# Two-layer graph network on one core: sums of sub-blocks for the second layer formed two units ahead instead of one

## What is computed

```python
def _L0_gnn_ref(h, adj, W_neigh, b_neigh, W_self, b_self):
    deg = jnp.sum(adj, axis=1, keepdims=True) + 1e-05
    h_neigh = (adj / deg) @ h
    return relu(h_neigh @ W_neigh.T + b_neigh + h @ W_self.T + b_self)

def _L1_gnn_ref(x, adj, W, b):
    rowsum = adj.sum(axis=1)
    d = jnp.where(rowsum > 0, rowsum ** (-0.5), 0.0)
    return relu((d[:, None] * adj * d[None, :]) @ x @ W + b)

x = layernorm(x + _L0_gnn_ref(x, adj, ...))      # x: 4096 x 256, adj: 4096 x 4096, all fp32
x = layernorm(x + _L1_gnn_ref(x, adj, ...))
```

## Time and profile before

| | |
|---|---|
| Median of three runs | 785.76 us |
| The profiled execution's own time | 786.03 us |
| Its span, first to last instruction | 784.3 us |
| TensorE, matmul | 769.7 us busy (98%) |
| VectorE (DVE) | 719.4 us busy (92%) |
| ScalarE (ACT) | 422.7 us busy (54%) |
| DMA | 161.09 MB, mean 205 GB/s |
| Granted TensorE clock, mean | 0.995 |

### The profile page before, as it was taken

One profiled execution on the slowest core, in us unless ns is written; L12 is line 12 of the kernel. 1 busy time (PEld: TensorE's weight loads), 2 busy tenths in 40 slices (PEclk: granted clock), 3 DMA queues, 4 the chain that ended last, 5 costly groups with the idle time before them and its releaser, 6 DMA issues.

```text
span 784.3 us, 12479 instructions
## 1 busy us (share of the span) xinstructions
PE 769.7 (98%) x4050; PEld 658.7 (84%) x4050; DVE 719.4 (92%) x1221; ACT 422.7 (54%) x590; POOL 2.6 (0%) x14
## 2 busy tenths in 40 slices
PE   9999999999999999999999999999999999999996
PEld 6888888888888888888888789898888889888886
DVE  6999999999899998999979999998999989899754
ACT  5644644646356463554535646555564665656452
POOL 0000000000000000000000000000000000000000
PEclk9999999999999999999999999999999999999998
DMA  8966574746547466474564655657465565745751
GB/s 299 340 237 196 198 253 164 256 170 213 215 164 249 174 198 231 152 249 170 203 232 155 196 186 189 242 170 260 146 219 202 182 241 166 277 146 192 269 164 52
DMA packets 54206, 161.09 MB, mean 205 GB/s; under 512 B 5024, under 2 KB 18080, under 8 KB 54176
## 3 DMA queue, kind: packets, MB, share of 16 engines
q1 hardware_dynamic: 45680, 151.54, 55.6%
q10 hardware_dynamic: 8352, 9.05, 3.7%
q0 software_dynamic: 144, 0.13, 0.1%
HBM read 152.31 MB, written 8.39 MB: 205 GB/s over the span
## 4 chain that ended last, share of the span: by engine, by line
PE 63%; DVE 19%; issue 10%; ACT 5%; DMA 2%; DVEq 1%; ACTq 0%; SPq 0%
PE ps_main L1091 51%; PE ps_epi L967 5%; DVE lo L565 4%; DVE acc L745 2%; DVE xs L565 2%; PE ps_main L1113 1%; ACT tt L405 1%; DMA raw<-adj_t 1%; DVE acc L742 1%; ACT xs L358 1%; DVE tt L643 1%; ACT hi L358 1%; DVE tt L635 1%; DVE tt L622 1%; DVE ps_main L708 1%
## 5 line engine op out<-in xcount | busy, mean ns | idle before, releaser
L358 ACT ACTIVATE hi<-raw 128x1024 fp32r<-128x1024 f32 x254 | 255.2, 1018 | 139.2 <-PE ps_main L1091 102.4
L565 DVE TENSOR_TENSOR lo<-raw,hi 128x1024 fp32r<-128x1024 f32 x254 | 298.0, 1175 | 21.7 <-ACT hi L358 21.6
L1091 PE MATMUL ps_main<-hi,xs 128*128 128x512 f32 x1120 | 278.9, 391 | 0.4 <-DVE xs L685 0.4
L1091 PEld LDWEIGHTS ps_main<-hi,xs 128*128 128x128 f32 x1120 | 207.4, 188 | 42.5 <-DVE xs L685 0.9
L1091 PE MATMUL ps_main<-lo,xs 128*128 128x512 f32 x560 | 149.7, 389 | 0.0
L848 DVE TENSOR_TENSOR acc<-acc,raw 128x1024 f32<-128x1024 f32 x112 | 136.4, 1218 | 0.0
L1091 PE MATMUL ps_main<-hi,zs 128*128 128x512 f32 x544 | 135.5, 391 | 0.0
L1091 PEld LDWEIGHTS ps_main<-lo,xs 128*128 128x128 f32 x560 | 105.1, 188 | 21.9
L1091 PEld LDWEIGHTS ps_main<-hi,zs 128*128 128x128 f32 x544 | 99.5, 188 | 18.9
L358 ACT ACTIVATE xs<-acc 128x1024 fp32r<-128x1024 f32 (+1 forms) x47 | 49.4, 1051 | 105.0 <-DVE acc L747 92.6
L1091 PE MATMUL ps_main<-lo,zs 128*128 128x512 f32 x272 | 72.7, 389 | 0.0
(11 more groups left out here) (159 smaller groups left out, 786.3 us busy)
## 6 DMA issues: line engine op xcount, KB each, us to landing
raw<-adj_t SPq DMA_DIRECT2D x256, 512.0 KB, 3.3
res<-x_nat SPq DMA_DIRECT2D x11, 512.0 KB, 5.9
xt_sb<-xt SPq DMA_DIRECT2D x8, 512.0 KB, 5.9
x_scratch<-tt ACTq DMA_DIRECT2D x8, 512.0 KB, 4.6
res<-x_scratch SPq DMA_DIRECT2D x8, 512.0 KB, 5.3
out<-tt ACTq DMA_DIRECT2D x7, 512.0 KB, 4.8
tt<-x_nat SPq DMA_DIRECT2D x3, 512.0 KB, 4.8
acc<-x_nat ACTq DMA_DIRECT2D x1, 512.0 KB, 5.1
```

The lines of the kernel that those rows point to most:

```text
L358: return act.activation(dst, src, ACT.Copy)
L565: return dve.tensor_tensor(dst, src, hi_part.bitcast(f32), ALU.subtract)
L1091: last = pe.matmul(ps[:, f, :], stationary(layer, part, jt, f), mov[:, slot(u), cols], start=(jt == 0 and i == 0), stop=(jt == JT - 1 and ...
```

## The change

```diff
@@ -42,6 +42,7 @@
 WARM = 10
 SU = tuple(range(1, 14, 2))
 NS = len(SU)
+SUMS_AT = tuple(max(u - 2, 0) for u in SU)
 SRING = 2
 T_AT = XC + FH
 T_UNITS = tuple(range(5, 16, 3))
@@ -825,8 +826,8 @@
                     if by_seven(layer, b):
                         if u in SU:
                             s_lo(b, parity, u)
-                        if u + 1 in SU:
-                            s_sums(b, parity, u + 1)
+                        if u in SUMS_AT:
+                            s_sums(b, parity, SU[SUMS_AT.index(u)])
                     if layer == 1 and is_first(b):
                         if u in T_UNITS:
                             t_lo(T_UNITS.index(u))
```

## The result

The changed kernel takes 799.32 us (median of four runs, 796.51 to 800.71) against 786.06 us for the kernel before. The ratio is 1.0165 with a 95% interval of 1.0134 to 1.0196: slower by 13.3 us, where 787.9 (785.9 to 790.0) was forecast. The change was forecast at 2.1 us, so the size was off by a factor of about six. The traced execution took 796.51 us, span 794.8 us, 10.5 us more than the traced one before.

The account below looks back on a forecast made before the run. VectorE's loop between `st_lo` waits was taken as the bound. Block 1's 1.6, block 3's 0.95 and 0 elsewhere gave +2.55 on 786.03, so 788.6; less 0.27 and weighted for runs without late landings, 787.9 us, range 785.9 to 790.0.

Parts of the forecast that it names:

- What bounds the kernel: Second layer: VectorE's loop between `st_lo` waits sets block length, 46.42 us; TensorE is busy 45.30, gains capped near 1.1.
- Cover in the middle of the block: Even units' `lo` comes 1.46 us later; tightest, unit 10, keeps 0.6 us before TensorE needs it; cost nothing.
- Small gaps: VectorE's dependent pairs, no longer separated by sums, each pay 0.11 us: 0.11 ahead of `st_lo`, 0.33 ahead of line 680.
- ScalarE's gain at the boundary: Block's end: earlier sums let ScalarE scale sooner; unit 14's 0.70 us wait goes, unit 15's stays; net gain 0.6 us.
- The load of unit 3: Unit 1, blocks 2, 4, 5, 6: tile takes 5.2 us, early read waits 0.5; ordinary block nets 0.0 us.
- Block 1: Unit 3's tile lands at 451.56 regardless; VectorE stands still 2.0 us and line 708 starts 1.6 us later.
- Late landings in single blocks: One of five tiles late, block 3 (6.9 us): +0.95 us there; a late landing costs 1.7 us instead of 0.7.
- TensorE's clock: Dip expected behind block 1's 2.8 us wait, absorbed by spare time; at most 0.6 us if in block 5 or 6.
- The rule from the pages: Unit 3's load estimated at 3.2 us, against 5.2 in rows; basis of the third rival, 783.2 us, chance 0.06.

Follow-up runs that it names:

- the residual late: Changed kernel with the residual's load in the second layer's blocks 1 to 6 issued after unit 4's tile instead of unit 2's; 789.58 us, ratio 1.0048.
- without the store: Changed kernel without the stores of the second layer's blocks 0 to 5; 790.41 us in one run.
- ScalarE delayed: Changed kernel with one added 128x512 copy on ScalarE between the scaling and `hi` of unit 14, some 0.6 us; 796.86 us in one run.
- the second trace: The changed kernel itself, unaltered, run and traced once more; 799.24 us, span 797.5.
- unit 3 alone: Kernel before the change with only unit 3's sums moved, from unit 2 to unit 1; 792.34 us, ratio 1.0080.
- unit 13 back: Changed kernel with unit 13's sums alone put back into unit 12; 795.20 us, ratio 1.0128.

## Why the prediction was wrong

The direction came out as forecast, but that is luck in the traced run: of the two terms that made the forecast slower, block 1 gave nothing there and a late landing was no longer the exception. The whole loss stands in the blocks that were forecast at no change.

**What bounds the kernel: right.** The distance of the waits for `st_lo` is what moved, and it accounts for 10.47 of 10.5 us in the traced run.

**Cover in the middle of the block: right.** Unit 10's `lo` ends 0.5 to 0.6 us before TensorE takes it up where no dip of the clock has put TensorE back (blocks 1, 3, 4 and 6), against 0.6 forecast. One weight load waits 0.3 us for `lo` of unit 2 in block 2, behind the 3.40 us in which VectorE stood still.

**Small gaps: right.** 0.45 us between 695 and 698.

**ScalarE's gain at the boundary: right,** 0.70 us before unit 14's `lo` gone, 0.71 before unit 15's still there. A block of the changed kernel closes with it: 46.44 - 0.6 + 0.1 + 2.53 = 48.5, and block 4 is 48.57 us long.

**The load of unit 3: the step that failed.** "Since the issue hangs on the same list, it moves with it, and the 0.5 stays whatever is won before it." The issue did move with it. The landing didn't stay 5.2 us. I had named both shifts that made it longer, unit 12's `lo` 1.46 us later with the load behind it and the boundary 0.6 us earlier, and asked of each only whether its own tile would be in time: "The loads have about 3.3 us and are needed four units later, about 10 us; nothing either." No engine waited for the moved one, the tile of unit 0. Its cost fell on others: the loads of units 0 and 1 came 1.4 us apart, store and residual ran into them, and the tile of unit 3 behind these landed 2.0 us later than the 5.2 of the sum in four blocks and 3.0 later in block 2. The runs with the residual late, without the store and with ScalarE delayed each took part of this away. What the five waits have beyond the forecast 0.5 us sums to 10.5 us (13.0 less 2.5), the size of the loss of the traced run. It isn't the whole account: some 0.1 us a block is left over, and block 3's 0.7 us of late landing in the kernel before pays for it.

**Block 1: not in the traced run, right in others.** +1.6 was forecast with a wait of 2.0. In the traced run the wait was 0.44 and the first wait for `st_lo` ended where it had before (457.88 against 457.86): nothing. It was 1.94 in the second trace and 2.21 with unit 3 alone. In the first trace the residual's load, which waits for the first layer's last store, was issued at 444.9 in place of 446.4.

**Late landings in single blocks:** in the kernel before one of five, as read. That one now costs all of its delay is borne out by block 2, whose tile landed 1.0 us later than block 3's and whose wait was 1.0 us longer. None of the size of 1.7 us came, and they are small beside the shift of all.

**TensorE's clock: dips came, but not by the wait's length.** See below. In the traced run they stood behind the waits of blocks 2 and 5; the one forecast for block 1 came in the second trace, where that wait was 2.85 us. They cost nothing at the end in the traced run, as forecast: behind the dip in block 2 block 3's wait is 1.74 us and not 3. The bound of 0.6 us for a late dip was too low: the one behind block 6's wait, with ScalarE delayed, cost 1.5.

**The rule from the pages.** The Trainium skill, page "DMA: Bandwidth & Descriptors", section "Anatomy of one DMA" for the software path, gives a fixed part and one for the bytes, an estimate of 3.2 us for 512 KB. These tiles go by SyncE's queue, which the profile lists as hardware. The traces agree even so for most tiles issued with nothing else in flight (3.0 to 3.5 us) and give up to 8.2 us for the same tile in the bunch. The Trainium skill, same page, section "Issuing engines are not separate DMA queues", says that DMAs started by different engines end up on the same 16 DMA engines and interleave. The run without the stores agrees: a store on ScalarE's queue cost unit 3's tile on SyncE's 0.7 to 2.4 us. The prediction didn't weigh this.

## What to carry to other kernels

When an edit moves the instruction that frees a buffer, write down the issue times of all transfers around the tightest one, before and after, and not only whether the moved one is in time: here a load took 3.3 us alone and 7 to 8 in the bunch. A read that is moved ahead by some time needs its tile's landing to have that time to spare in every block, and here it had 1.0 us where 1.5 were wanted; with the tile late as well, that one read made 11.3 of the 13.3 us. And the cheapest remedy was in no engine's arithmetic: a transfer that isn't urgent (the residual, in block 4 issued at 587.8 and first read at 612.3) goes behind the one that is.

## What the runs showed of the hardware

A delay among loads can be handed on: after two issues 0.9 us apart, loads 2.7 us apart keep landing after 4.2 us, while those after a pause of 4 us (579.4 to 583.4 in the changed kernel) are back at 3.2. It can fade too, as it did ahead of block 2 in the kernel with unit 13 back.

The granted clock after TensorE's wait isn't told by the length of the wait (windows of the changed kernel behind block 2's wait of 3.96 us and block 4's of 3.27: length, busy PE, PEld, DVE, ACT, POOL, clock, DMA, GB/s):

```profile
507.32:511.32 4.00, 4.00 (x17) 3.61 (x18) 3.96 (x8) 2.73 (x4) 0.00 (x0) 0.59 0.30 120
...
604.40:609.40 5.00, 5.00 (x34) 4.63 (x35) 4.97 (x10) 3.73 (x5) 0.00 (x0) 1.00 0.28 98
```

After 3.96 us it fell to the 1.2 GHz level for most of the stretch, after 3.27 us it stayed at 2.4 GHz, while in the kernel before 1.83 us were enough for a fall. What decides it, these traces don't show.
